# A graph network layer: destination degrees counted from run lengths on the chip, in place of a gather per tile

## The reference

```python
src = concatenate([edge_index[0], loop]); dst = concatenate([edge_index[1], loop])
deg = segment_sum(ones_like(dst), dst, num_segments=N)
dinv = where(deg > 0, rsqrt(deg), 0.0)
norm = dinv[src] * dinv[dst]
H = X @ W
msgs = H[src] * norm[:, None]
out = segment_sum(msgs, dst, num_segments=N) + b
return where(out >= 0, out, NEG_SLOPE * out)
```

## Time and profile before

| | us |
|---|---|
| median of 3 runs | 1536.49 |
| lowest and highest run | 1533.14, 1540.46 |
| the profiled execution, its own time | 1538.9 |
| its span, first to last instruction | 1537.1 |
| mean granted TensorE clock, of full speed | 0.950 |

### The profile page before, as it was taken

The page is one execution under the profiler, slowest core; times in us unless marked ns, Lnnn a source line. Parts: engine busy times, 40 slices in busy tenths (PEclk is TensorE's granted clock), DMA queues, the critical chain, the costliest instruction groups (busy, mean ns, idle before and its releaser), DMA issues. The chain is left out here.

```text
span 1537.1 us, 25199 instructions
## 1 busy us (share of the span) xinstructions
PE 1365.4 (89%) x7928; PEld 1148.8 (75%) x7928; DVE 1104.1 (72%) x2041; ACT 611.4 (40%) x1155; POOL 828.3 (54%) x814
## 2 busy tenths in 40 slices
PE   1788886999999939999999999999999996388798
PEld 1788785888877829999999999999999985243344
DVE  4454543688888842678888888888888887465677
ACT  1465553455555531322332322322223331255566
POOL 2777773566666543465555555555565542333444
PEclk8798998999999969999999999999999997698999
DMA  3577765576666542344444554544444435657764
GB/s 123 188 259 238 238 206 202 175 225 217 221 218 225 199 137 76 97 131 130 130 135 131 137 137 140 152 140 123 123 123 123 126 108 189 197 180 238 251 192 162
DMA packets 124328, 259.00 MB, mean 168 GB/s; under 512 B 22089, under 2 KB 22537, under 8 KB 124144
## 3 DMA queue, kind: packets, MB, share of 16 engines
q1 hardware_dynamic: 92528, 176.89, 36.4%
q0 software_dynamic: 31200, 80.40, 17.1%
q10 hardware_dynamic: 544, 1.05, 0.2%
HBM read 198.24 MB, written 73.61 MB: 177 GB/s over the span
## 5 line engine op out<-in xcount | busy, mean ns | idle before, releaser
L173 PE MATMUL pse<-w_lo,w_hi 128*128 128x256 f32 (+1 forms) x1440 | 467.2, 324 | 25.4 <-DVE w_lo L1106 20.4
L174 PE MATMUL pse<-w_hi,w_lo 128*128 128x256 f32 (+1 forms) x1440 | 462.7, 321 | 0.0
L175 PE MATMUL pse<-w_hi 128*128 128x256 f32 (+1 forms) x1440 | 462.5, 321 | 0.0
L173 PEld LDWEIGHTS pse<-w_lo,w_hi 128*128 128x128 f32 x1440 | 277.6, 193 | 46.3 <-issue 21.4
L175 PEld LDWEIGHTS pse<-w_hi 128*128 128x128 f32 x1440 | 277.2, 192 | 20.2
L174 PEld LDWEIGHTS pse<-w_hi,w_lo 128*128 128x128 f32 x1440 | 277.7, 193 | 18.8
L937 POOL TENSOR_TENSOR acc_x<-acc_x,node_rows 128x512 f32<-128x512 f32 (+1 forms) x79 | 125.5, 1588 | 76.4 <-DMA node_rows<-x_table 71.8
L663 POOL TENSOR_TENSOR node_y<-node_z,node_x 128x512 f32<-128x512 f32 x79 | 101.9, 1290 | 100.0 <-issue 79.5
L1308 POOL DMA_INDIRECT rows_over_w_lo<-msg_table,last_edge x79 | 85.0, 1076 | 111.0 <-ACT rows_over_w_lo L1340 97.0
L528 DVE TENSOR_TENSOR_SCAN run<-goes_on,run,psa 128x128 f32<-128x128 f32 (+1 forms) x156 | 62.2, 461 | 93.5 <-PE psa L560 89.1
L174 PE MATMUL psn<-w_hi,agg_lo 128*128 128x512 f32 x316 | 125.3, 396 | 0.0
(11 more groups left out here) (198 smaller groups left out, 2932.5 us busy)
## 6 DMA issues: line engine op xcount, KB each, us to landing
coef_all<-coef_table SPq DMA_DIRECT2D x40, 512.0 KB, 6.9
node_x<-in_x SPq DMA_DIRECT2D x79, 256.0 KB, 2.8
x_table<-node_x SPq DMA_DIRECT2D x79, 256.0 KB, 2.0
node_rows<-x_table SPq DMA_DIRECT2D x79, 256.0 KB, 7.2
rows_over_w_hi<-x_table SPq DMA_DIRECT2D x12, 1024.0 KB, 6.6
edge_part<-part SPq DMA_DIRECT2D x20, 512.0 KB, 3.7
sum_table<-sums SPq DMA_DIRECT2D x40, 256.0 KB, 4.5
part_in<-edge_part SPq DMA_DIRECT2D x20, 512.0 KB
```

The source lines that it names most:

```text
L173: pe.matmul(to, left[0], right[1], start=first, stop=False)
L174: pe.matmul(to, left[1], right[0], start=False, stop=False)
L175: return pe.matmul(to, left[0], right[0], start=False, stop=last)
```

## The change

The factor by which L502 scales the run sums needs no exact `dinv` for every edge, only for the last edge of each run, since only that row of `sum_table` is used later. There, the number of edges of the run up to and with this edge is the number of all edges of the destination. So the 40 `dinv_dst` gathers are dropped, with column 4 of `edge_idx`, and at the head of the aggregation stage the position in its run is computed for every edge, plus one for the loop, and from it 1/sqrt with a Newton step.

A further copy of the flags, `goes_flat`, holds one tile to a partition (40 x 128). One scan counts along each tile from zero, a second tells whether a run has gone on since the tile's start. The last columns of both are turned into rows by TensorE, a scan over the 40 tiles gives what each tile carries over from the ones before, that is turned back into a column and added, and the counts are transposed to 128 x 40. ScalarE takes the square root, VectorE does the rest. TensorE, ScalarE and VectorE each do this ahead of their loop; `deg_step` counts the 11 steps. The wait at L491 counts two gathers instead of three, and the first L502 waits for the end of the chain.

```diff
--- before.py
+++ after.py
@@ -152,7 +152,7 @@
         g.dinv = sb(whole, "dinv", [P, NT])
         g.dinv_sq = sb(whole, "dinv_sq", [P, NT])
         g.last_edge = sb(whole, "last_edge", [P, NT], I32)
-        g.edge_idx = sb(whole, "edge_idx", [P, ET, 5], I32)
+        g.edge_idx = sb(whole, "edge_idx", [P, ET, 4], I32)
         g.is_last = sb(whole, "is_last", [P, ET])
         g.br_col = sb(whole, "br_col", [P, K])
         g.bv_col = sb(whole, "bv_col", [P, K])
@@ -176,6 +176,7 @@
 
         with ExitStack() as early:
             g.goes_on = sb(early, "goes_on", [P, EP], BF16)
+            g.goes_flat = sb(early, "goes_flat", [ET, P], BF16)
             g.sb, g.sem, g.banks, g.w, g.product = sb, sem, banks, w, product
             g.w_half, g.load_half = w_half, load_half
             index_stage(nc, g)
@@ -260,11 +261,12 @@
                 sp.dma_start(g.goes_row[0:1, 0:1], same[0:1, P:P + 1]).then_inc(row_in, 16)
                 sp.dma_start(g.goes_row[0:1, 1:EP + 1].rearrange("a (t p) -> (a t) p", p=P), same[:, 0:P]).then_inc(row_in, 16)
                 sp.wait_ge(row_in, 32)
+                sp.dma_start(g.goes_flat[:], g.goes_row[0:1, 0:EP].rearrange("a (t p) -> (a t) p", p=P)).then_inc(stored, 16)
                 sp.dma_start(g.goes_on[:], g.goes_row[0:1, 0:EP].to_broadcast([P, EP])).then_inc(stored, 16)
                 sp.wait_ge(dinv_ok, 1)
                 sp.dma_start(g.dinv_table.rearrange("(p j) c -> p (j c)", p=P), g.dinv[:]).then_inc(stored, 16)
                 sp.wait_ge(const_in, 32)
-                sp.wait_ge(stored, 64)
+                sp.wait_ge(stored, 80)
 
             @block.scalar
             def _(act):
@@ -396,7 +398,6 @@
                 v.tensor_copy(g.edge_idx[:, :, 1], cols_s[:, 1, :])
                 v.scalar_tensor_tensor(g.edge_idx[:, :, 2], low[:, 1, :], float(NT), high[:, 1, :], ALU.mult, ALU.add)
                 v.tensor_copy(g.edge_idx[:, :, 3], cols_s[:, 0, :])
-                v.scalar_tensor_tensor(g.edge_idx[:, :, 4], low[:, 0, :], float(NT), high[:, 0, :], ALU.mult, ALU.add)
                 dve.wait_ge(hist_ok, 1)
                 v.tensor_copy(cnt[:], ps[2][:, 0:NT]).then_inc(cnt_ok, 1)
 
@@ -433,7 +434,12 @@
         x_rows = sb(ctx, "x_rows", [P, R, D])
         scaled = sb(ctx, "scaled_rows", [P, 2, D])
         dinv_src = sb(ctx, "dinv_src", [P, R, 1])
-        dinv_dst = sb(ctx, "dinv_dst", [P, ET, 1])
+        dinv_dst = sb(ctx, "dinv_dst", [P, ET])
+        count = sb(ctx, "run_count", [ET, 2, P])
+        carried = sb(ctx, "count_carried", [1, ET + 1])
+        whole = sb(ctx, "count_goes_through", [1, ET])
+        carry = sb(ctx, "count_carry", [ET, 1])
+        deg = sb(ctx, "dst_degree", [P, 4, ET])
         ea_hi = sb(ctx, "ea_hi", [P, 2, K, BE], F32R)
         ea_lo = sb(ctx, "ea_lo", [P, 2, K, BE], F32R)
         run = sb(ctx, "run", [P, R, K, P])
@@ -451,6 +457,8 @@
         g.row_out = row_out
         r_mm, part_ok, part_out = sem("edge_part_in_psum"), sem("edge_part_ready"), sem("edge_part_out")
 
+        deg_step = sem("dst_degree_step")
+        RUNS, ENDS, CARRIED, CARRY_TURNED, COUNTED, TURNED, DEGREES, ROOTS, DINV_DST = 2, 4, 5, 6, 7, 8, 9, 10, 11
         w_in = [sem(f"weights_in{s}") for s in range(2)]
         w_hi_ok, w_lo_ok = sem("later_weights_high"), sem("later_weights_low")
 
@@ -473,10 +481,12 @@
                     wait(pool, scaled_ok, t - R + 1)
                     rows_of(g.x, x_rows[:, s, :], t, 1).then_inc(x_in[s], 16)
                     rows_of(g.dinv_table, dinv_src[:, s, :], t, 2).then_inc(x_in[s], 16)
-                    rows_of(g.dinv_table, dinv_dst[:, t, :], t, 4).then_inc(x_in[s], 16)
 
             @block.scalar
             def _(act):
+                act.wait_ge(deg_step, DEGREES)
+                nc.scalar.activation(deg[:, 1, :], deg[:, 0, :], ACT.Sqrt).then_inc(deg_step, 1)
+
                 def step(j, s, on):
                     for q in range(2):
                         if on(0):
@@ -487,7 +497,7 @@
                     for q in range(2):
                         if on(0):
 
-                            act.wait_ge(x_in[2 * s + q], 3 * landed(j, s, 0, 2))
+                            act.wait_ge(x_in[2 * s + q], 2 * landed(j, s, 0, 2))
                             wait(act, x_t, 2 * (j - 1) + q + 1)
                             nc.scalar.activation(scaled[:, q, :], x_rows[:, 2 * s + q, :], ACT.Copy, scale=dinv_src[:, 2 * s + q, :]).then_inc(scaled_ok, 1)
                     if on(1):
@@ -499,7 +509,9 @@
                         for q in range(2):
                             act.wait_ge(back_ok, 2 * (j - 1) + q + 1)
                             wait(act, row_out[q], 16 * (j - 1))
-                            nc.scalar.activation(sums[:, q, :], ps_back[q][:], ACT.Copy, scale=dinv_dst[:, bass.ds(2 * (j - 1) + q, 1), :].rearrange("p t c -> p (t c)")).then_inc(row_ok, 1)
+                            if isinstance(j, int) and j == 1:
+                                act.wait_ge(deg_step, DINV_DST)
+                            nc.scalar.activation(sums[:, q, :], ps_back[q][:], ACT.Copy, scale=dinv_dst[:, bass.ds(2 * (j - 1) + q, 1)]).then_inc(row_ok, 1)
                     if on(0, LATER):
                         wait_alone(act, w_in[s], landed(j, s, 0, 2), g.passed)
                         nc.scalar.copy(g.w_half(g.w_hi, j + 2), w_stage[:, s, :]).then_inc(w_hi_ok, 1)
@@ -508,6 +520,32 @@
             @block.vector
             def _(dve):
                 v = nc.vector
+                steps = g.steps
+
+                def then(ins):
+
+                    steps[0] += 1
+                    ins.then_inc(g.step_v, 1)
+                    dve.wait_ge(g.step_v, steps[0])
+
+                v.memset(carried[:, 0:1], 0.0)
+                v.tensor_tensor_scan(count[:, 0, :], g.goes_flat[:], g.ones[0:ET, :], 0.0, ALU.mult, ALU.add).then_inc(deg_step, 1)
+                v.tensor_tensor_scan(count[:, 1, :], g.goes_flat[:], g.ones[0:ET, :], 1.0, ALU.mult, ALU.mult).then_inc(deg_step, 1)
+                dve.wait_ge(deg_step, ENDS)
+                then(v.tensor_copy(whole[:], ps_back[1][0:1, 0:ET]))
+                v.tensor_tensor_scan(carried[:, 1:], whole[:], ps_back[0][0:1, 0:ET], 0.0, ALU.mult, ALU.add).then_inc(deg_step, 1)
+                dve.wait_ge(deg_step, CARRY_TURNED)
+                then(v.tensor_copy(carry[:], ps_back[0][0:ET, 0:1]))
+                v.scalar_tensor_tensor(count[:, 0, :], count[:, 1, :], carry[:, 0:1], count[:, 0, :], ALU.mult, ALU.add).then_inc(deg_step, 1)
+                dve.wait_ge(deg_step, TURNED)
+                v.tensor_scalar(deg[:, 0, :], ps_back[1][:, 0:ET], 1.0, None, ALU.add).then_inc(deg_step, 1)
+                dve.wait_ge(deg_step, ROOTS)
+                y, half = deg[:, 2, :], deg[:, 3, :]
+                then(v.reciprocal(y, deg[:, 1, :]))
+                then(v.tensor_tensor(half, y, y, ALU.mult))
+                then(v.tensor_tensor(half, half, deg[:, 0, :], ALU.mult))
+                then(v.tensor_scalar(half, half, -0.5, 1.5, ALU.mult, ALU.add))
+                v.tensor_tensor(dinv_dst[:], y, half, ALU.mult).then_inc(deg_step, 1)
 
                 def step(j, s, on):
                     for q in range(2):
@@ -534,6 +572,15 @@
 
             @block.tensor
             def _(pe):
+                pe.wait_ge(deg_step, RUNS)
+                for i in range(2):
+                    pe.transpose(ps_back[i][0:1, 0:ET], count[:, i, P - 1:P], g.ident[0:ET, 0:ET]).then_inc(deg_step, 1)
+                pe.wait_ge(deg_step, CARRIED)
+                pe.transpose(ps_back[0][0:ET, 0:1], carried[:, 0:ET], g.ident[0:1, 0:1]).then_inc(deg_step, 1)
+                pe.wait_ge(deg_step, COUNTED)
+                pe.transpose(ps_back[1][:, 0:ET], count[:, 0, :], g.ident[0:ET, 0:ET]).then_inc(deg_step, 1)
+                pe.wait_ge(deg_step, DEGREES)
+
                 def step(j, s, on):
                     if on(0):
                         for q in range(2):
```

## The result

| us | before | after |
|---|---|---|
| median | 1537.83 (4 runs, 1533.14 to 1540.46) | 1499.29 (4 runs, 1496.84 to 1500.87) |
| profiled execution, its own time | 1538.9 | 1500.35 |
| its span | 1537.1 | 1498.5 |
| mean granted TensorE clock | 0.950 | 0.956 |

The ratio is 0.9748, with a 95% interval of 0.9723 to 0.9772: 38.5 us less by the medians. Forecast were 1501 us, with a range of 1493 to 1512.

The account below looks back on a forecast made before the run. GpSimd's gather issue was taken to bound the aggregation stage. Start, 18 shorter block periods and unchanged tail gave 35.6 us less: 1538.9 to 1503.3 profiled, so a median of 1501 us, range 1493 to 1512.

Parts of the forecast that it names:

- What bounds before: Aggregation stage: GpSimd saturated as an issuer; eight gathers at 1.29 us are 10.3 us, the period of a two-tile block.
- The periods: Aggregation blocks, mark to mark (start of a block's L560 transposes): from 10.24 us to 8.45 for 13, 8.3 for last five.
- The start: Aggregation stage up to the second block's L560 transposes: 57.0 us instead of 59.62, tile 3's edge rows asked for 3.75 earlier.
- The tail and the rest: From the last block's L560 transposes to the next stage's gathers: 14.9 us, unchanged, and so are the later stages.
- The sum: Twentieth block's L560 transposes at 57.0 + 13 x 8.45 + 5 x 8.3 = 208.4 us against 243.99: 35.6 us earlier.
- the rival of TensorE's floor: Aggregation blocks: all 18 periods at 8.26 us, last mark 39.3 us earlier, kernel 1497 us; chance 0.12.
- The costs taken as nothing: Degree chain under the wait for aggregation's first gather, 0 us (bounds 0 to 2.5); index stage's added transfer, 0.
- One sign of being wrong: Aggregation stage's start: first edge transposes later than 38.3 us would mean that the degree chain delays them.
- DMA as the bound: Aggregation stage: share held to 0.79, first 13 periods 9.25 us, mark 25 us earlier, kernel 1511 us; chance 0.15.
- The gathers hidden anyway: Aggregation stage: gathers were hidden, or the chain doesn't take their place cleanly; kernel about 1536 us; chance 0.04.
- The clock: Aggregation stage: TensorE's denser loop held at clock 0.50, 15.4 us a block, kernel about 1627 us; chance 0.03.
- GpSimd was to wait for buffers: Aggregation stage, profile after: a sign expected was GpSimd waiting for a buffer in some blocks, hardly there before.

## Why the prediction was right

**What bounds before.** Right, and shown from three sides: putting the gathers back undoes all of the gain, taking away the wait alone gives nothing, a fifth gather costs 1.21 us for each tile.

**The periods.** The 13 periods from the second mark to the fifteenth took (165.08 - 53.58) / 13 = 8.58 us, forecast 8.45; the last five 8.37, forecast 8.3. The size was nearly right but its make-up wasn't. The forecast put the excess over 8.26 us down to GpSimd and DMA in every block with weights. What happened is two things: four early periods of 9.0 us on average (8.60 to 9.79), in which GpSimd hadn't built up its lead (they are 8.37 when it has four gathers only), and nine of 8.37, TensorE's own, as the last five. Long gathers were there, one of 1.81 to 1.88 us in each of the nine blocks from 94 to 161 us, and cost nothing once the lead stood. In that stretch GpSimd ran without a wait for a buffer and yet at exactly TensorE's 8.37 us. I read it so: a gather that comes earlier meets more of the subtraction and is held longer, which ties GpSimd's pace to VectorE's; no run was made for that alone. The excess over 0.945 us is 124.0 - 113.4 = 10.6 us, more than the 7.0 of before, and none of it shows in the late marks.

**The start.** This is the term most in error: second mark at 53.58, forecast 57.0 with 55.9 as the early end. The rows:

```profile
46.60 1.20 DVE L570 TENSOR_TENSOR w_lo<-w_stage_later,w_hi 128x1024 fp32r<-128x1024 f32 x1
46.66 1.95 POOL L475 DMA_INDIRECT dinv_src<-dinv_table,edge_idx  x1 [0.30 <-issue]
...
47.34 0.66 PE L590 MATMUL psa<-ident,ea_rows 128*128 128x128 f32 x4 [2.05 <-DMA ea_rows<-in_ea,edge_idx]
...
47.95 0.28 PE L174 MATMUL psa<-ea_hi,w_lo 128*128 128x256 f32 x1
```

The first of the 48 products began at 47.75, and all but that one took 0.28 us each, as at 2.4 GHz, where they took 0.41 in the earlier trace rows. The forecast had TensorE begin them at the lower level, either as before or with the rise moved along with the work. In this execution the clock was at 0.53 in the window from 44 to 46 us and at 1.00 in the next, behind only the transposes. That isn't so in every execution. In the second profile of the changed kernel the ten products from 48.59 to 50.51 took 0.41 or 0.42 us again, and the level rose behind them:

```profile
50.51 0.42 PE L174 MATMUL psa<-ea_hi,w_lo 128*128 128x256 f32 x1
...
51.01 0.28 PE L174 MATMUL psa<-ea_hi,w_lo 128*128 128x256 f32 x1
```

The mark came at 55.19 there. The window from 48 to 50 us of that profile shows a granted clock of 1.00 all the same, so there the length of the products tells the level and the window's clock doesn't. So 1 to 2 us of the earlier mark are luck, but they aren't worth much: in the second profile the last mark was only 0.30 us later (207.24), for its early periods were shorter (8.37, 9.62, 8.46 and 8.38 us). A fast start is partly given back while GpSimd has no lead. The work began on time, too: the transposes of tile 3 came at 47.34, forecast 47.4, with a gather of 1.95 us beside the subtraction just ahead of it, whose data TensorE doesn't need yet.

**The tail and the rest.** 14.91 us, forecast 14.9. The later stages were left at what they were, and were 1.6 us shorter.

**The sum.** 243.99 - 206.94 = 37.05 us, forecast 35.6: 3.4 more from the start, 2.0 less from the periods (111.5 + 41.9 us against 109.9 + 41.5). That the sum came within 1.5 us is in part luck: the two errors have opposite signs and, as said, hang together. The result lies at the edge between the forecast (31 to 38 us) and the rival of TensorE's floor (over 38): 38.5 us by the two medians, 37.2 against the 1536.49 that the forecast started from. That rival, which had a chance of 0.12, described the late blocks better.

**The costs taken as nothing.** Right: without the chain the time is the same. One sign of being wrong did show, first transposes later than 38.3 us, which was to mean the chain: they came at 38.58. But without the chain they came at 38.47, so 0.1 us at most shows as the chain's, and the bound was set closer than executions differ. VectorE was done with it at 36.61, forecast 38, TensorE with its last transpose at 34.7, forecast 35.5. No table load came with the square root, which took 0.24 us for 40 columns.

**The rivals.** DMA as the bound had 0.15; 376 GB/s with TensorE undisturbed show that it wasn't near. The step that misled was to take the highest share of a long window, 0.79, in a kernel bound by something else, for a possible limit; the earlier trace rows has 0.89 and 325 GB/s over 5 us. The gathers hidden anyway: refuted by the result. The clock: 1.00 from 60 to 200 us, so with the denser work the falls of the earlier trace rows are gone and no others came.

**What was to be seen and wasn't.** GpSimd was to wait for buffers in some blocks; it did so once, at 187 us, for 0.30 us. The DMA share is 0.91, not 0.85. For the blocks with weights the forecast took 236 GB/s and 0.71, the window with the lowest rate of those that have them; over whole periods before it is 251 GB/s and 0.75, 7.7 us of DMA time for a block, and 7.7 / 8.45 is 0.91.

## What to carry to other kernels

A queue that issues small gathers has a price for each instruction, here 1.25 us for 512 bytes, whatever it moves; count the instructions of such a queue over the stage. If they fill it without a break and the other engines wait for what they bring, that engine is the bound though its busy share is 0.77. The first sign alone isn't enough: in the changed kernel GpSimd's queue ran on without a break too, and TensorE was the bound; what told was that TensorE had stopped waiting, and that two gathers fewer in a block left its late blocks as they were. The wait which the profile names longest may only be the place where an engine stands: before trusting it, ask whether the engine behind the awaited transfer was idle at any time. And when the bound moves, look for the shortest period in the trace of before, in which the data happened to be there: it gave the new period within 1.5%.

## What the runs showed of the hardware

A gather that GpSimd begins while VectorE subtracts two large SBUF inputs lasted until about 0.8 us after that instruction's end (106.83 for 106.01, 48.61 for 47.80), up to 2.00 us in all; beside a tensor_scalar of 0.67 us with one small SBUF input, up to 1.48. Beside VectorE's instructions with an input in PSUM gathers took the usual 0.95 us. A share of DMA time of 0.91 doesn't mean that 9% is left: a fifth more traffic, 376 for 312 GB/s, went through in the same time. TensorE's products at 2.4 GHz had a pitch of 0.117 to 0.120 us, which differed between layouts and also within one execution (before: 0.1175 from 100 to 109 us, 0.120 from 117 to 121); what sets it wasn't found.
